# From graph 3 on: neighbour lists in ranks, a degree pass of its own, DVE instead of PE for the scores, and SyncE instead of POOL for the table

## The reference

```python
def _L0_gnn_ref(A, X, W, b):                      # S = 25
    mask = A != 0
    scores = jnp.where(mask, -jnp.arange(N), neg_inf)
    vals, idx = jax.lax.top_k(scores, S)          # the neighbours, lowest first
    feats = jax.vmap(lambda x, i: x[i])(X, idx)
    agg = where(valid, feats, neg_inf).max(axis=2)
    ...
    return relu(concatenate([X, agg]) @ W + b)
def _L1_gnn_ref(x, adj, edge_types, W, a1, a2, edge_emb, ln_gamma, ln_beta):
    Wh = x @ W                                    # 8 heads of 32
    e = s1[:, :, None, :] + s2[:, None, :, :] + edge_emb[edge_types]
    alpha = softmax(where(adj == 0, -1e9, leaky(e)))
    h = alpha @ Wh
    return elu(layernorm(h) * ln_gamma + ln_beta)
x = _layernorm(x + _L0_gnn_ref(adj, x, ...))
x = _layernorm(x + _L1_gnn_ref(x, adj, adj, ...))
```

## Time and profile before

| | |
|---|---|
| three runs | 4688.99, 4660.63, 4616.15 us, median 4660.63 |
| profiled execution | 4624.79 us, its span 4623.0 us |
| mean granted TensorE clock | 0.683 of full speed |
| busy, share of the span | POOL 56%, DVE 49%, PE 44%, ACT 21% |
| device memory | 475.54 MB read, 52.95 MB written |

### The profile page before, as it was taken

One profiled execution on the slowest core, in us unless ns is written; L12 is line 12 of the kernel. 1 busy time (PEld: TensorE's weight loads), 2 busy tenths in 40 slices (PEclk: granted clock), 3 DMA queues, 4 the chain that ended last, 5 costly groups with the idle time before them and its releaser, 6 DMA issues.

```text
span 4623.0 us, 23616 instructions
## 1 busy us (share of the span) xinstructions
PE 2015.0 (44%) x4938; PEld 981.9 (21%) x4939; DVE 2285.4 (49%) x5645; ACT 988.1 (21%) x2222; POOL 2590.5 (56%) x2723
## 2 busy tenths in 40 slices
PE   6365453434445344443453443444444323434443
PEld 1133231111222122221221221222222111212111
DVE  6564554545545455464454544545445334335445
ACT  3121132211222122221122221222212111112123
POOL 2655555574565655664655546556455664665653
PEclk9976666766666666676666666666666656666666
DMA  5544433443344333443334333343332332332321
GB/s 192 193 161 164 131 127 109 134 121 94 114 126 134 116 106 113 139 125 100 114 113 146 111 104 111 117 132 115 108 96 83 96 93 72 89 94 78 90 80 49
DMA packets 201351, 530.24 MB, mean 115 GB/s; under 512 B 65521, under 2 KB 99314, under 8 KB 184818
## 3 DMA queue, kind: packets, MB, share of 16 engines
q0 software_dynamic: 128256, 357.70, 26.3%
q1 hardware_dynamic: 72946, 170.98, 10.8%
HBM read 475.54 MB, written 52.95 MB: 114 GB/s over the span
## 4 chain that ended last, share of the span: by engine, by line
another core or an unknown queue 36%; PE 17%; DVE 17%; issue 14%; ACT 9%; DVEq 4%; POOL 2%; DMA 1%; ACTq 0%; SPq 0%; POOLq 0%
PE att_p L760 8%; DVE ring L1149 4%; DVEq L867 4%; PE lin_p L726 4%; ACT adj_h L561 3%; DVE cand L1033 3%; DVE agg L991 2%; ACT L607 2%; POOL ring L497 1%; PE lin_p L724 1%; PE wh_p L740 1%; DVE agg L984 1%; PE score_p L693 1%; PE score_p L694 1%
## 5 line engine op out<-in xcount | busy, mean ns | idle before, releaser
L760 PE MATMUL att_p<-ring,ident 128*128 128x512 f32 (+2 forms) x1248 | 814.4, 818 | 1720.3 <-DVE ring L1149 1442.1
L497 POOL DMA_INDIRECT ring<-table_d,idx_loc x1128 | 1074.3, 952 | 680.7 <-issue 351.7
L497 POOL DMA_INDIRECT ring<-in_x_dram,idx_cur x1128 | 1081.7, 959 | 503.9 <-issue 339.4
L760 PEld LDWEIGHTS att_p<-ring,ident 128*128 128x128 f32 (+1 forms) x1248 | 324.2, 272 | 2164.4 <-DVE ring L1149 1483.6
L1112 DVE SCALAR_TENSOR_TENSOR z<-lin_p,xs 128x256 f32<-128x256 f32 x128 | 54.3, 424 | 899.7 <-remote 714.4
L512 POOL DMA_INDIRECT out_dram<-res,own_out x128 | 128.0, 1000 | 592.1 <-DVE res L870 545.6
L991 DVE TENSOR_REDUCE agg<-ring 128x256 f32<-128x2560 f32 (+9 forms) x120 | 453.0, 3775 | 0.0
L726 PE MATMUL lin_p<-w_s,h_t 128*128 128x256 f32 x1024 | 394.2, 552 | 0.0
L596 ACT ACTIVATE att_s<-att_p 128x256 f32<-128x256 f32 x128 | 49.1, 383 | 1497.4 <-PE att_p L760 694.5
L1033 DVE MAX8 cand<-score_p 128x8 f32<-128x256 f32 x848 | 291.3, 414 | 79.0 <-remote 72.7
L585 ACT ACTIVATE tab<-wh_p 128x264 f32<-128x264 f32 x128 | 49.9, 390 | 1302.3 <-remote 977.1
(11 more groups left out here) (150 smaller groups left out, 2661.1 us busy)
## 6 DMA issues: line engine op xcount, KB each, us to landing
adj_i<-in_adj_dram SPq DMA_DIRECT2D x128, 1024.0 KB
ring<-in_x_dram,idx_cur POOLq DMA_INDIRECT x1128
ring<-table_d,idx_loc POOLq DMA_INDIRECT x1128
pay<-in_x_dram SPq DMA_DIRECT2D x8, 2048.0 KB
xs<-sorted_d SPq DMA_DIRECT2D x128, 128.0 KB
sorted_d<-pay,rank_i POOLq DMA_INDIRECT x128
idx_cur<-sorted_d SPq DMA_DIRECT2D x8, 256.0 KB
table_d<-tab,idx_loc POOLq DMA_INDIRECT x128
```

The lines of the kernel that those rows point to most:

```text
L497: pool.indirect_dma_start(out=to[:, k * width:(k + 1) * width], out_offset=None, in_=source, in_offset=bass.IndirectOffsetOnAxis(ap=idx_at ...
L760: last = pe.matmul(att_p[:, 0:n * C], ident[0:on, :], r3[0:on, s:s + n, 0:C], start=(s == 0), stop=(s + 2 >= k))
```

## The change

It does five things. **Search:** `scores` on PE goes. DVE multiplies the cast tile `adj_h` by a row of codes that stands in PSUM on every partition as bf16 (`mark`, one tensor_tensor of 128x2048 into the new SBUF buffer `marked`), and takes the maxima from `marked`. The codes are bf16 numbers whose bits fall by one from column to column. `mark(n + 1)` stands in round r's steps between the last statistics and `bn_aggr`; the maxima stand where they stood. **Degree pass:** for graphs 3 to 7 each adjacency tile is loaded a second time and earlier (`DAHEAD`, 41 rounds ahead of layer 0), and ACT sums its degrees alone, by a cast that overwrites `adj_i` (80 more loads of 1 MB, 80 more casts; they stand behind `exps` in the round). **Ranks first:** for these graphs the sort is made from the degrees before the search starts, and each column's code is made from its rank (`rank_rows`, 16 PE transposes in `codes`), so the lists hold ranks from the start. **Sources:** layer 0 of these graphs gathers from `sorted_d` and not from `x`. **Table:** since the lists name ranks, `table_d` is stored in order, by a plain DMA of SP (`store_table`), and the 80 `scatter_table` of POOL go. Graphs 0 to 2 keep their lists in node numbers and their table scatters, but are marked by DVE as well. Fewer constants are made at the start.

```diff
+RANKED = 3
+DAHEAD = AHEAD + T + 3
...
+def order_casts():
+    order = [("search", n) for n in range(AHEAD + 2)]
+    of_round = []
+    for r in range(ROUNDS):
+        start = len(order)
+        if r + AHEAD + 2 < TILES:
+            order.append(("search", r + AHEAD + 2))
+        if RANKED * T <= r + DAHEAD < TILES:
+            order.append(("degree", r + DAHEAD))
+        of_round.append(range(start, len(order)))
+    return order, of_round
+CASTS, CASTS_OF = order_casts()
+CAST_AT = {c: k for k, c in enumerate(CASTS)}
+def sorted_in(r):
+    n, d = r + AHEAD, r + DAHEAD - 1
+    if 0 <= n < RANKED * T and n % T == T - 1:
+        return n // T
+    if RANKED * T <= d < TILES and d % T == T - 1:
+        return d // T
+    return None
+SORTS = [0] + [sorted_in(r) for r in range(ROUNDS) if sorted_in(r) is not None]
...
+            def store_table(i):
+                b, u = tile0(i)
+                sp.wait_ge(tab_ready, i + 1)
+                sp.dma_start(table_d[b][u * P:(u + 1) * P, :], tab[i % 4][:, :]).then_inc(tab_st[i % 4], 16)
...
             for r in range(ROUNDS):
                 if first(r + 1):
                     load_self(r + 1)
-                if first(r + AHEAD + 4):
-                    load_adj(r + AHEAD + 4)
+                if first(r - 1) and (r - 1) // T >= RANKED:
+                    store_table(r - 1)
+                for k in CASTS_OF[r]:
+                    if k + 2 < len(CASTS):
+                        load_adj(k + 2)
...
+            step(pool.iota(cols_i, pattern=[[-1, N]], base=FIRST, channel_multiplier=0))
+            step(pool.tensor_scalar(cols_i, cols_i, 65536.0, None, ALU.mult))
...
-                source, width = (table_d[b], ROW) if layer else (x_rows, C)
+                width = ROW if layer else C
+                source = table_d[b] if layer else x_rows if b < RANKED else sorted_d[b]
...
-                if first(r - LAG0):
+                if first(r - LAG0) and (r - LAG0) // T < RANKED:
...
-            def cast(n):
-                q = n % 2
-                act.wait_ge(adj_ld[q], 16 * (n // 2 + 1))
-                if n < AHEAD + 3:
-                    need(act, score_ready, 2 * n - 2)
-                act.activation(adj_h[q][:, :], adj_i[q][:, :], ACT.Copy,
-                               accum_out=degree[:, n:n + 1]).then_inc(cast_done, 1)
+            def cast(k):
+                kind, n = CASTS[k]
+                q = k % 2
+                act.wait_ge(adj_ld[q], 16 * (k // 2 + 1))
+                if kind == "degree":
+                    act.activation(adj_i[q][:, :].bitcast(F32), adj_i[q][:, :], ACT.Copy,
+                                   accum_out=degree[:, n:n + 1]).then_inc(cast_done, 1)
+                    return
+                need(act, cast_used, n - 1)
+                if n < RANKED * T:
+                    act.activation(adj_h[n % 2][:, :], adj_i[q][:, :], ACT.Copy,
+                                   accum_out=degree[:, n:n + 1]).then_inc(cast_done, 1)
+                else:
+                    act.activation(adj_h[n % 2][:, :], adj_i[q][:, :], ACT.Copy).then_inc(cast_done, 1)
...
-                if first(r + AHEAD + 2):
-                    cast(r + AHEAD + 2)
+                for k in CASTS_OF[r]:
+                    if CASTS[k][0] == "search":
+                        cast(k)
...
+                if sorted_in(r) is not None:
+                    totals(sorted_in(r))
+                for k in CASTS_OF[r]:
+                    if CASTS[k][0] == "degree":
+                        cast(k)
                 roots(r)
...
-            def scores(n):
-                q = n % 2
-                if n < AHEAD + 3:
-                    pe.wait_ge(cast_done, n + 1)
-                need(pe, score_used, 2 * n)
-                for h in range(2):
-                    for c in range(2):
-                        o = score_p[h][:, 512 * c:512 * (c + 1)]
-                        at = slice(1024 * h + 512 * c, 1024 * h + 512 * (c + 1))
-                        pe.matmul(o, mark_h[:, :], adj_h[q][:, at], start=True, stop=False)
-                        last = pe.matmul(o, ones_h[0:64, :], cols_h[:, at], start=False, stop=True)
-                    last.then_inc(score_ready, 1)
...
+            def codes(g):
+                pe.wait_ge(code_put, g - RANKED + 1)
+                for c in range(T):
+                    last = pe.transpose(code_of(g)[:, P * c:P * (c + 1)],
+                                        code_h[:, c:c + 1].broadcast_to([P, P]), ident_h[:, :])
+                last.then_inc(code_ready, 1)
...
+            def mark(n):
+                dve.wait_ge(cast_done, CAST_AT["search", n] + 1)
+                if n >= RANKED * T and n % T == 0:
+                    dve.wait_ge(code_ready, n // T - RANKED + 1)
+                v.tensor_tensor(marked[:, :], adj_h[n % 2][:, :], code_of(n // T), ALU.mult).then_inc(cast_used, 1)
+            def chunks():
+                for c in range(8):
+                    v.max(cand[:, 8 * c:8 * c + 8], marked[:, CH * c:CH * (c + 1)])
...
+            def degree_codes(g):
+                settle()
+                if g >= RANKED:
+                    dve.wait_ge(cast_done, CAST_AT["degree", g * T + T - 1] + 1)
                 v.tensor_scalar(degc[:, :], degree[:, g * T:(g + 1) * T], float(DCODE - 1), None, ALU.min)
-                v.tensor_scalar(f3[:, :, 0:WIDEST], l3[:, :, 0:WIDEST], MARK, None, ALU.is_gt)
-                settle()
-                v.tensor_reduce(found[:, :], f3[:, :, 0:WIDEST], AX, ALU.add)
+                settle()
                 v.tensor_tensor(onehot[:, :].rearrange("p (d t) -> p d t", t=T),
                                 degc[:, :].unsqueeze(1).broadcast_to([P, DCODE, T]),
                                 drev[:, :].unsqueeze(2).broadcast_to([P, DCODE, T]), ALU.is_equal)\
                     .then_inc(onehot_ready, 1)
+            def rank_rows(g):
+                settle()
+                dve.wait_ge(rank_ready, SORTS.index(g) + 1)
+                v.tensor_tensor(rprod[:, :], turn_p[:, :], onehot[:, :], ALU.mult).then_inc(rank_used, 1)
+                settle()
+                v.tensor_reduce(rank[:, :], rprod[:, :].rearrange("p (d t) -> p t d", t=T), AX, ALU.add)
+                settle()
+                need(dve, list_out, 16 * T * (g - 1))
+                last = v.tensor_copy(rank_i[g % 2][:, :], rank[:, :])
+                if g < RANKED:
+                    last.then_inc(pay_ready, 1)
+                else:
+                    v.tensor_scalar(code_i[:, :], rank[:, :], -65536.0, 65536.0 * FIRST, ALU.mult, ALU.add)
+                    settle()
+                    v.tensor_copy(code_h[:, :], code_i[:, :].bitcast(F32)).then_inc(code_put, 1)
...
                 if first(n):
-                    for h in range(2):
-                        dve.wait_ge(score_ready, 2 * n + h + 1)
-                        for c in range(4):
-                            at = 8 * (4 * h + c)
-                            last = v.max(cand[:, at:at + 8], score_p[h][:, CH * c:CH * (c + 1)])
-                        last.then_inc(score_used, 1)
+                    chunks()
...
                     v.bn_stats(stats[:, 12:18], y2[:, :])
+                if first(n + 1):
+                    mark(n + 1)
                 settle()
```

More of the change, by code:

```diff
@@ L52 @@
 X1_KEPT = 38
-CONSTS0 = 7
-CONSTS = 46
+CONSTS0 = 2
+CONSTS = 43
 def tile0(i):
@@ L126, in build @@
         rank = sb("rank", [P, T])
-        rank_i = sb("rank_i", [P, T], I32)
+        rank_i = [sb(f"rank_i{q}", [P, T], I32) for q in range(2)]
+        code_i = sb("code_i", [P, T], I32)
+        code_h = sb("code_h", [P, T], BF16)
         pay = sb("pay", [P, T * SENT])
@@ L211, in build @@
         lin_p = pb("lin_p", [P, 2 * C])
+        code_p = [score_p[q][:, :].bitcast(BF16) for q in range(2)]
         wh_p = pb("wh_p", [P, 2 * C])
@@ L246, in build @@
         tab_out = [sem(f"tab_out{q}") for q in range(4)]
+        tab_st = [sem(f"tab_st{q}") for q in range(4)]
         xsum_ready = sem("xsum_ready")
@@ L762, in attend @@
                 last.then_inc(att_ready, 1)
-            pe.wait_ge(consts_done, CONSTS0)
-            for n in range(T):
-                scores(n)
             pe.wait_ge(consts_done, CONSTS)
@@ L769, in _ @@
             ranks(0)
-            for n in range(T, AHEAD + 1):
-                scores(n)
             pe.wait_ge(weights_ld, 16 * 8)
@@ L775, in _ @@
                 j = r - LATER
-                n = r + AHEAD
                 if first(r):
-                    for g in range(1, B):
-                        if (r - 1 + AHEAD) == T * g + T - 1:
-                            pe.wait_ge(rank_used, g + 1)
+                    g = sorted_in(r - 1)
+                    if g is not None:
+                        pe.wait_ge(rank_used, SORTS.index(g) + 1)
+                        if g >= RANKED:
+                            codes(g)
                     if r == 0:
@@ L793, in _ @@
                     mean(j // T)
```

(20 more changed lines are left out.)

126 lines of the change are left out of this document (64 added, 62 removed).

## The result

The changed kernel takes 4507.6 us (median of 4 runs, 4474.6 to 4517.9) against 4641.0 us of the kernel before (4 runs): ratio 0.9714, interval 0.9667 to 0.9761, so 133 us or 2.9% faster. The forecast was 4530, its range 4420 to 4660. Ratios and their intervals leave out the executions in which the chip was in a slower state; medians are over all. The profiled execution took 4517.92 us, with a span of 4516.1.

A forecast was written before the change was run, and what follows sets the result against it. PE's semaphore signals, held up while POOL issues indirect DMAs without pause, were taken to set the pace. Scatters -91, marks +19 and scores -25 gave -97 us on 4624.8, 4528, forecast as 4530; range 4420 to 4660.

The forecast's parts named there:

- What bounds the kernel: Rounds: POOL's burst of two rounds, 3 to 6 us until PE's late signals, 14 us of DVE to `res`; 30 us a round.
- Scatters, -91 us: POOL's bursts: 80 table scatters leave at 1.30 us each, 104 us, nearly all on the path; -91 us.
- the bursts come apart: Rival: POOL pauses over 2 us each round, signals arrive in time, half the narrow rounds gain 260 us; 4365 us, chance 0.12.
- Marks, +19 us: DVE between late signal and `res`: 128 multiplications at 1.23 us, partly absorbed by idle time; +19 us.
- scores, -25 us: DVE's 56.6 us wait for PE's score signals goes, half of it while POOL stands; -25 us.
- the slow mark: Rival: DVE's mark takes 2.29 us, one element a cycle; 4576 us, or up to 4615, chance 0.22.
- unchanged within 30: Sign: the stage of graphs 0 to 2 keeps its length within 30 us.
- Degree pass, 0: ACT's 80 casts of 1.9 us are covered, and 80 MB more loads don't slow POOL's DMAs; 0 us.
- Ranks first, the other source, 0: Ranking moves to another round, its sixteen transposes due one round later, 0 us; no term for the gathers' source.
- the unknown queue: Sign: this chain item, 36% before, stays about a third; below a fifth, POOL's runs of DMAs have broken up.
- the scatters were no cost: Rival: POOL's gathers wait for ring space, so removing scatters gains nothing; -6 us, 4619 us, chance 0.08.
- DVE takes over: Rival: mark at 2.29 us, POOL pauses briefly every round, signals stay late, every mark exposed; +103 us, 4728 us, chance 0.08.

The follow-up runs named there:

- 4 to 8: Stop of POOL behind layer 0's gathers: changed kernel with twelve memsets 0.9419, drain 0.8931, four memsets 0.8979, wait for PE 0.9033; kernel before, twelve memsets 0.9716.
- 10: Kernel before with only a drain of POOL behind layer 0's gathers: 4225.2 us, ratio 0.9134.
- 11: Changed kernel with a drain of POOL behind layer 1's gathers, ahead of the output's scatter: 4112.1 us, ratio 0.8886.
- experiment 2: Changed kernel with the tables of graphs 3 to 7 stored by POOL's indirect DMAs again instead of SP: 4686.7 us, ratio 1.0010.
- Experiment 9: Changed kernel with all tables stored by POOL and a drain of POOL behind layer 0's gathers in each round: 4234.8 us, ratio 0.9151.
- experiment 1: Changed kernel with RANKED = 8: DVE's marks only, lists in node numbers, no degree pass, all 128 table scatters on POOL: 4663.0 us, ratio 0.9953 to the kernel before.
- experiment 3: Marks-only kernel plus the degree pass as dead load, 80 more loads and casts with unused sums: 4659.2 us, ratio 0.9956 to the kernel before.

## Why the prediction was right, and where it was off

**What bounds the kernel** was read rightly, and is now shown and not only argued: 4 to 8, 10 and 11 add nothing but stops of POOL (a drain, memsets or a wait), and make the kernel 3 to 9% faster. That the signals are on time early in POOL's run and late far into it is in the counts above: the prediction's "about 16 us" lies where it changes. Why a stop is needed for PE's signals is not settled by these runs, and how a late signal turns into lost time is argued from POOL's wait for `res`.

**Scatters, -91 us:** the step that was mis-sized. They are worth 137 us (113 to 161, experiment 2), more than their whole issue time of 104. The forecast priced them inside bursts that keep their shape, at their issue time less what lies under a wait. The counts show that part as 67 us in graphs 3 to 6. Where the rest comes from stays open. The rival "the bursts come apart" had 260 us for half of the narrow rounds, all or nothing; the five to seven short stops that the changed kernel has more than the others would fit a small part of it, and the sum had no term for such a part. Experiment 9, with a stop in each round, gives 102 us for the 80 scatters, which would fit too, but its uncertainty reaches 137.

**Marks, +19 us, and scores, -25 us:** together -22 (-36 to -8, experiment 1) against -6. The mark's 1.23 us, taken from a row with other operands, measured 1.21; the slow mark is out. Of the Trainium skill's two sentences in VectorE: DVE Perf Modes, the one in "Why PSUM operands drop a tier" holds here: the mark, with one bf16 operand in PSUM, took the 1.2 us of two elements a cycle. The tier table's entry for tensor_tensor with any PSUM operand, about 2.3 us, doesn't hold for it. In the searches at the start the step went from 5.98 to 5.77 us, and layer 0 began 13 us earlier, where -2 and -3 had been put down. In graphs 0 to 2 I had said "unchanged within 30" and it was +35: +15 in graph 0, -1.5 in graph 1, +21 in graph 2. Exposed marks were foretold for the first rounds alone, by POOL's wait for `tab`, and these executions don't show them: graph 0 takes 296 us before and from 291 to 324 us in the traces with marks. Why graph 2 is longer, with sorts and searches of later graphs in its rounds, is open. That the maxima no longer wait is seen; that later signals of PE move up in their queue isn't, or is small.

**Degree pass, 0:** right, by experiment 3, to within some 19 us.

**Ranks first, the other source, 0:** between experiments 3 and 2 lie 0.0054, +25 us, with an uncertainty of 16. It can be the sixteen transposes and the sort in another round, or the gathers from `sorted_d`. POOL doesn't issue these more slowly: they take 955 to 958 ns each, and those from `x` 952 to 965 in the traces. No run separates the two. The prediction took the transposes at nothing and had no term for the other source; this stays open.

The four steps, -22 + 0 + 25 - 137 = -134, give the -133 of the comparison by construction, since each is the difference of two neighbours in one chain of kernels; that they add up confirms none of them. The forecast's -97 is 36 us short of it: its largest term was too small by 46 us, and the others were too kind by 9. That the forecast time of 4530 came within 22 us of the measured 4508 is partly luck: it was counted from an execution of 4625 us, and the kernel before had its median at 4641. Of what would show it: the unknown queue at 29% of the chain came out, and so did POOL's 48 stops before `out_dram` (their mean was 11 us before and is 11 now; the "near 18" was that of the rounds shown). The later graphs became 18, 25, 30 and 33 us shorter each, where 15 to 25 had been said, as an undersized term for the scatters would have it.

**The rivals:** "the scatters were no cost" fell with experiment 2. "The slow mark" fell with the row of `marked`, 1.2 us, and "DVE takes over" needed it. "The bursts come apart", at 4365 us, did not happen: the unknown queue stayed at 29%, above the fifth that was its sign.

## What to carry to other kernels

When the chain's largest item is a wait for a signal whose sender has long been done, look at what another engine does at that time, and test it by making that engine stop for a moment; here that was worth about three times the change itself. An instruction taken out of an unbroken run on the engine that sets the pace can be worth more than its own duration (here 137 us against 104), so give such a term room upward, and look for what the length of the run decides. Work on engines that wait anyway (80 MB of loads, 153 us of casts, even each mark a second time) cost nothing that these runs can measure.

## What the runs showed of the hardware

- PE's semaphore signals reach DVE up to some 28 us late (`z0`) and ACT up to some 35 us late (`tab`) while POOL issues indirect DMAs every 1.25 us without a break. In the first 12 us of such a run 1 signal of 56 for `z0` was late, beyond 20 us 30 of 31. The held signals come one by one while POOL goes on, or mostly 2 to 6 us after it stops. With a drain between them two indirect DMAs of POOL lie 3.2 to 3.9 us apart in most rounds, where it is 0.30 without, and that is stop enough; so is a wait of POOL for a signal of PE. The cause of the delay is open.
- DVE itself stalls, with nothing that the profile shows it to wait for: before the last maximum of the lists by up to 3.7 to 4.4 us, 107 us in 42 times in the changed kernel (L1157), 92 us in 37 times before (L1085), 78 us in 40 times with the drain behind layer 0's gathers and 29 us in 22 times with it behind layer 1's. It is there without the degree pass too (121 us in 44 times with marks alone, 132 us in 45 with the pass); the cause is open.
- A tensor_tensor of 128x2048 with bf16 in SBUF, bf16 in PSUM and bf16 out takes 1.21 us. Maxima over 256 elements take 0.41 us from PSUM in float32 and from SBUF in bf16 alike.
